# Macaron block: TensorE's implied waits left out of attention, and one quarter copy of v moved from ScalarE to VectorE

## The reference

```
qkv = x @ Wqkv.T + bqkv                       # x after a layer norm; 16 heads of 16
q = (elu(q) + 1 + 1e-4) / 4
k = elu(k) + 1 + 1e-4
num = q . cumsum(k v^T);  den = q . cumsum(k) + 1e-4
out = (num / den) @ Wout.T + bout             # then layer norm, gamma, beta
x = x + out
```

## Time and profile before

| | |
|---|---|
| time, median of 3 runs | 2193.14 us (2190.23 to 2194.28) |
| time of the profiled execution | 2192.45 us |
| its span, first to last instruction | 2190.7 us |
| granted TensorE clock, mean share of full speed | 0.994 |
| steps of attention read, 830 to 1394 us | 103 of 128 |

### The profile page before, as it was taken

One profiled execution on the slowest core, in us unless ns is written; L12 is line 12 of the kernel. 1 busy time (PEld: TensorE's weight loads), 2 busy tenths in 40 slices (PEclk: granted clock), 3 DMA queues, 4 the chain that ended last, 5 costly groups with the idle time before them and its releaser, 6 DMA issues.

```text
span 2190.7 us, 91337 instructions
## 1 busy us (share of the span) xinstructions
PE 2101.8 (96%) x30384; PEld 1506.7 (69%) x30384; DVE 2044.7 (93%) x5231; ACT 1930.6 (88%) x4136; POOL 1905.6 (87%) x3002
## 2 busy tenths in 40 slices
PE   3899999999999999999999999979999999999998
PEld 1566666666666688888888888864666666666665
DVE  7999999999999788999999999978999999999997
ACT  7888888888888789999999999978888888888885
POOL 5899999999999778888888888878999999999996
PEclk9999999999999999999999999999999999999999
DMA  4765555555555432222222222223555555555555
GB/s 103 130 121 117 116 115 116 115 115 114 114 114 110 85 57 59 61 61 61 61 61 61 61 61 61 61 45 72 121 115 116 116 114 114 114 114 116 115 119 116
DMA packets 719856, 208.74 MB, mean 95 GB/s; under 512 B 666400, under 2 KB 719520, under 8 KB 719776
## 3 DMA queue, kind: packets, MB, share of 16 engines
q1 hardware_dynamic: 719776, 207.76, 46.8%
HBM read 20.38 MB, written 16.78 MB: 17 GB/s over the span
## 4 chain that ended last, share of the span: by engine, by line
PE 88%; DVE 4%; issue 3%; ACT 2%; DMA 2%; POOL 1%; SPq 0%; POOLq 0%; ACTq 0%; DVEq 0%
PE ffn_ps_gu L861 39%; PE ffn_ps_down L873 21%; PE attn_ps_qk L1265 7%; PE attn_ps_sc L1318 5%; PE attn_ps_num L1305 4%; PE attn_ps_v_second L1281 3%; PE attn_ps_z L1345 3%; PE attn_ps_num L1310 2%; PE attn_ps_kT_first L1272 1%; PE attn_ps_z L1342 1%; PE attn_ps_kT_first L1333 1%; DMA attn_xT<-attn_x_hl 1%; DVE ffn_y L759 1%; DVE ffn_per_block L721 0%; PE attn_ps_v_second L1333 0%
## 5 line engine op out<-in xcount | busy, mean ns | idle before, releaser
L861 PE MATMUL ffn_ps_gu<-wgu_hi,ffn_xT 128*128 128x512 f16 (+1 forms) x3072 | 740.6, 364 | 14.5 <-DVE ffn_hx L710 6.2
L861 PEld LDWEIGHTS ffn_ps_gu<-wgu_hi,ffn_xT 128*128 128x128 f16 x3072 | 301.6, 98 | 302.4 <-issue 22.4
L861 PE MATMUL ffn_ps_gu<-wgu_lo,ffn_xT 128*128 128x512 f16 (+1 forms) x1536 | 432.9, 364 | 0.0
L791 POOL TENSOR_TENSOR ffn_h_hl<-ffn_q,ffn_h_scale_hi 128x704 f16<-128x704 f16 x256 | 352.5, 1377 | 28.2 <-DVE ffn_q L751 8.9
L807 ACT ACTIVATE ffn_quarter<-ffn_y,offsets 128x960 int16<-128x960 f32 (+2 forms) x264 | 282.5, 1070 | 99.2 <-DVE ffn_y L759 97.0
L873 PE MATMUL ffn_ps_down<-wd_hi,ffn_hT 128*128 128x256 f16 x2816 | 349.3, 273 | 10.0 <-DVE x_sb L735 6.0
L792 POOL TENSOR_TENSOR ffn_h_hl<-ffn_q,ffn_h_scale_lo 128x704 f16<-128x704 f16 x256 | 355.3, 1388 | 0.0
L873 PEld LDWEIGHTS ffn_ps_down<-wd_hi,ffn_hT 128*128 128x128 f16 x2816 | 274.5, 98 | 71.1 <-issue 9.4
L721 DVE TENSOR_REDUCE ffn_per_block<-ffn_hx 128x60 f32<-128x960 f32 (+2 forms) x264 | 298.0, 1129 | 5.4
L759 DVE TENSOR_TENSOR ffn_y<-ffn_hx,ffn_per_block 128x960 f32<-128x960 f32 (+2 forms) x264 | 292.4, 1108 | 0.0
L843 ACT ACTIVATE ffn_odd<-ffn_quarter,offsets 128x960 f16<-128x960 int16 (+2 forms) x264 | 278.7, 1056 | 10.8 <-POOL ffn_shift L786 10.8
(11 more groups left out here) (184 smaller groups left out, 5236.5 us busy)
## 6 DMA issues: line engine op xcount, KB each, us to landing
x_sb<-in_L_attn_x SPq DMA_DIRECT2D x128, 128.0 KB, 2.5
out<-x_sb SPq DMA_DIRECT2D x128, 128.0 KB, 2.1
attn_v_eo<-attn_v_nat SPq DMA_DIRECT2D x256, 34.0 KB, 1.8
ffn_xT<-ffn_x_hl SPq DMA_TRANSPOSE x256, 2.5
ffn_hT<-ffn_h_hl SPq DMA_TRANSPOSE x256, 3.5
attn_xT<-attn_x_hl SPq DMA_TRANSPOSE x128, 2.4
attn_oT<-attn_o_hl SPq DMA_TRANSPOSE x128, 2.5
x_sb<-in_L_ffn_w_gate SPq DMA_DIRECT2D x2, 352.0 KB, 5.0
```

The lines of the kernel that those rows point to most:

```text
L791: nc.gpsimd.tensor_tensor(blocks(h_hl[par][:, 0:INNER]), blocks(q[par][:, 0:INNER]), over_block(h_scale_hi[par][:], HB), ALU.mult)
L861: last = nc.tensor.matmul(ps_gu[par][:, a:b], xT[par][:, c, :], w[:, k, a:b], start=(n == 0), stop=(n == len(terms) - 1))
```

## The change

In TensorE's step most waits are left out where another wait of the same step implies them. Before `kT` the wait for `feat` stays only where no tile i + 1 exists. Before v the waits for `v_nat` and `kv_second` go. Before `num` ten waits (`mid`, `before`, `q_feat`, `placed`, `v_own`, `masked`, `o_ready`, `k_odd`, `q_rows`, `masked` of the tile before) become four, in the order `placed`, `mid`, `q_rows`, `masked`. Before `kv` the wait for `v_nat` and one increment of `turn` go. On ScalarE the quarter of the lower rows is copied no more, only that of the upper rows. VectorE makes the other copy, in front of `den`, and waits for `v_nat` of tile i + 1 and for `num_done` of the tile that used the buffer last.

```diff
@@ vector_step
                 nc.vector.scalar_tensor_tensor(zg[:], ps_z[:, 0:D], mv[oth][:, 2:3], rows[:, 1, :], ALU.subtract, ALU.mult).then_inc(S["z_gamma"], 1)
+            if valid(tf, N):
+
+                ready(dve, "v_nat", tf)
+                freed(dve, "num_done", tf, 2)
+                nc.vector.tensor_copy(v_eo[oth][half(0), 0, 0], v_nat[oth][half(0), 0]).then_inc(S["v_low"], 1)
             if valid(tm, N):
 
                 ready(dve, "num_done", tm)
@@ scalar_step
                 ready(act, "v_nat", tf)
                 freed(act, "num_done", tf, 2)
-                for a in range(2):
-                    last = nc.scalar.activation(v_eo[oth][half(a), a, a], v_nat[oth][half(a), a], ACT.Copy)
-                last.then_inc(S["v_own"], 1)
+                nc.scalar.activation(v_eo[oth][half(1), 1, 1], v_nat[oth][half(1), 1], ACT.Copy).then_inc(S["v_own"], 1)
@@ tensor_step
             if valid(i, N):
 
-                ready(pe, "feat", i)
+                if not valid(tf, N):
+                    ready(pe, "feat", i)
                 freed(pe, "kv_first", i, 1)
...
             if valid(tf, N):
 
-                if valid(i, N):
-                    ready(pe, "v_nat", i)
-                    if not (isinstance(i, int) and i == 0):
-                        pe.wait_ge(S["kv_second"], i)
                 for n, (aT, w, k) in enumerate(terms):
...
+                placed(pe, tn, oth)
                 ready(pe, "mid", tn)
-                if not (isinstance(tn, int) and tn == 0):
-                    pe.wait_ge(S["before"], tn)
-                ready(pe, "q_feat", tn)
-                placed(pe, tn, oth)
-                ready(pe, "v_own", tn)
+            if valid(i, N):
+                if not valid(tn, N):
+                    ready(pe, "k_odd", i)
+                ready(pe, "q_rows", i)
+            if valid(tn, N):
                 ready(pe, "masked", tn)
-                freed(pe, "o_ready", tn, 1)
-            if valid(i, N):
-                ready(pe, "k_odd", i)
-                ready(pe, "q_rows", i)
-                freed(pe, "masked", i, 1)
...
                 ready(pe, "k_nat", i)
                 pe.sem_inc(S["turn"], 1)
-                ready(pe, "v_nat", i + 1 if valid(tf, N) else i)
-                if not valid(tf, N):
-                    pe.wait_ge(S["kv_second"], N - 1)
-                pe.sem_inc(S["turn"], 1)
```

More of the change, by code:

```diff
@@ L879 @@
 ATTN_SEMS = ("sums", "stats", "var", "rstd", "shift", "xn", "x_hi", "x_split", "turn", "xT_even", "xT_odd", "qk_done", "relu", "exp", "feat", "k_even", "k_odd",
-             "q_feat", "q_rows", "v_done", "v_nat", "v_own", "v_eo_even", "v_eo_odd", "kT_done", "k_nat", "scores_done", "masked", "kv_done", "kv_first", "kv_second",
+             "q_feat", "q_rows", "v_done", "v_nat", "v_own", "v_low", "v_eo_even", "v_eo_odd", "kT_done", "k_nat", "scores_done", "masked", "kv_done", "kv_first", "kv_second",
              "mid", "before", "num_done", "den", "rden", "o_ready", "o_hi", "o_split", "oT_even", "oT_odd", "proj_done",
@@ L1286, in tensor_step @@
                     pe.wait_ge(F["y"], N + X_AHEAD)
+                placed(pe, tn, oth)
                 ready(pe, "mid", tn)
-                if not (isinstance(tn, int) and tn == 0):
-                    pe.wait_ge(S["before"], tn)
-                ready(pe, "q_feat", tn)
-                placed(pe, tn, oth)
-                ready(pe, "v_own", tn)
-                ready(pe, "masked", tn)
-                freed(pe, "o_ready", tn, 1)
-            if valid(i, N):
-                ready(pe, "k_odd", i)
-                ready(pe, "q_rows", i)
-                freed(pe, "masked", i, 1)
-            if valid(tn, N):
+            if valid(i, N):
[3 more added lines that the diff above has]
+            if valid(tn, N):
+                ready(pe, "masked", tn)
                 for c in range(DC):
```

## The result

The changed kernel takes 2199.79 us, median of 8 runs (2192.35 to 2204.41), against 2193.22 us for the kernel before, also 8 runs (2188.13 to 2194.79). The ratio is 1.0032, 95% interval 1.0021 to 1.0043: slower by 0.3%, where 2182 us was forecast. The profiled execution took 2199.45 us (span 2196.8).

A forecast was written before the change was run, and what follows sets the result against it. A dependence round through VectorE and the gap before `num` was the bound. Its new sum, 0.12 + 1.22 + 0.05 + 0.15 + 0.02 + 3.77 + 0.05 = 5.38, saves 10.4 us: 2192.45 to 2182, range 2170 to 2197.

The forecast's parts named there:

- The round of 5.47 us: Attention step before the change: gap after `masked` 0.43, `num` to `den` 1.22, `den` to `masked` 3.77, loop branch 0.05.
- Waits before `num`: TensorE ahead of `num`: gap after `masked` falls from 0.43 to 0.12 us, a gain of 0.31 a step.
- The copy's price: VectorE's copy ahead of `den`: 0.20 us a step, 0.05 for its wait and 0.15 start to start.
- The sum of 5.38: Attention step after the change, by the same round: 5.38 us, 0.09 less than before.
- The loop's term: VectorE's loop branch, ahead of `bn_stats`: 0.05 us a step.
- TensorE's 5.29 and ScalarE's 4.97: Attention step: TensorE's own floor, and ScalarE's busy time with one copy less, in us; both below the new step.
- the case that the rivals left at 0.05: A new stall, from the `oT` transposes or GpSimd's own round, on either side of the forecast; chance 0.05.
- the 115 steps: Steps counted as gaining 0.09 us each: the 103 read plus half of the other 25, 10.4 us in all.
- Rival C: GpSimd holds VectorE's copy by 0.22 us or all of `x_beta`: step 5.58, 13 us slower, 2205 us; chance 0.13.
- the 0.02 in the sum: Allowance in us a step for GpSimd holding up VectorE's copy ahead of `den`.
- "Hidden" waits: TensorE's waits left out before `kT`, v and `kv`, and one `turn` increment: worth zero, as matmuls still run meanwhile.
- ScalarE's relief: ScalarE loses one of two copies, 0.32 us a step: zero by itself, but removes what would have been the next bound.

The follow-up runs named there:

- before_oT_plain: The kernel before the change, with the DMA transpose of o replaced by a plain copy of the same tile: 2190.01 us, ratio 0.9988.
- waits_only: The changed kernel with ScalarE making both copies again, so only TensorE's waits are left out: 2182.92 us, ratio 0.9954.
- oT_plain: The changed kernel with the DMA transpose of o replaced by a plain copy of the same tile: 2182.20 us, ratio 0.9952.
- copy_only: The kernel before the change with one copy made by VectorE ahead of `den`, all of TensorE's waits kept: 2242.07 us, ratio 1.0219.
- no_low_copy: The changed kernel without VectorE's copy, so nobody copies that quarter of v and ScalarE makes one copy: 2185.75 us, ratio 0.9961.

## Why the prediction was wrong

**What bounds the kernel now: right.** The round of 5.47 us through VectorE and the gap ahead of `num` set the step before the change. before_oT_plain leaves the step at 5.48, so the other round was not in the way then.

**Waits before `num`: right.** The gap went from 0.43 to 0.14 or 0.15 (forecast 0.12) wherever `num` waits for `masked`. waits_only shows what this is worth, 10.5 us, together with the other waits left out.

**The copy's price: right in size.** The copy lasts 0.22 us, as the 225 ns of the prediction's working, and `den` starts 0.15 after the copy, as forecast; the estimate of 131 ns, which the prediction weighed against that 0.15, was 0.02 short. With the copy's wait, `num` to `den` grew from 1.22 (1101.75 to 1102.97) to 1.46 and 1.44 (1099.53 to 1100.99, 1104.89 to 1106.33), so by 0.22 to 0.24 where 0.20 was forecast.

**The sum of 5.38: right for the round it adds up.** oT_plain shows the changed kernel with the other round out of its way: 21.62 in four steps, 5.40 a step. That its time of 2182.20 us meets the forecast of 2182 as well is in part luck, since the same edit took 4 us from the kernel before without touching the step. The loop's term was a little small: `den` to the end of `masked` takes 4.03 in one step of four and 3.76 in the others, 0.07 a step for 0.05.

**The step that failed** is the sentence that followed: "It is still above TensorE's 5.29 and ScalarE's 4.97." The new round was held against the busy time of engines and not against other rounds of dependence. There was one, over four steps, through SyncE's queue and GpSimd. With waits and copy as changed it is 22.00 us long, 5.50 a step. In kind it is the case that the rivals left at 0.05 ("a new stall (the oT transposes, GpSimd's own round)") without a price. (22.00 - 21.62) / 4 = 0.095, and by the 115 steps that the prediction counts (its own estimate) this is 11 us of the 17.8 between forecast and result.

**Rival C came in part.** `x_beta` holds the copy, mostly by 0.6 us, in 7 of 128 steps, 3.9 us; this is 0.03 a step over all steps, near the 0.02 in the sum by luck, for nearly all other copies last 0.22. The prediction put the copy ahead of `shift`, and so of `x_beta`, which is true in three steps of four (1100.84 and 1101.16). In the fourth v is late, `num` is late with it, and the copy meets `x_beta` within 0.06 us. The number of held copies differs between the two profiled executions with the same steps otherwise (7 at 2199.45 us, 20 at 2207.71), so it can be a part of the spread of these kernels, 2192 to 2204 and 2192 to 2210 us. It isn't shown to be all: the kernel before, without this copy, spreads from 2188 to 2198 in 29 runs. The Trainium skill, "SBUF — State Buffer", section "Who interferes with whom", says that the order of issue decides which of the two is blocked; two pairs of rows agree: at 1155.86 the copy is first and `x_beta` takes 0.80 for 0.73, in copy_only `x_beta` is first by 0.08 (1065.71) and the copy takes 0.74 for 0.22. At 1265.84 the records begin 0.01 us apart, which is too close to tell from them which was issued first.

**What is left over.** Holds and the longer round make 15 of the 17.8 us; the rest was not taken apart. Between before and after as a whole, the steps from the 13th to the 121st `num` take 3.7 us more (834.35 to 1430.45 against 832.90 to 1425.33), the 12 steps ahead of them 1.2 and the 7 behind them 1.3.

**"Hidden" waits: right for this kernel, by luck.** They cost nothing in the changed kernel (22.01 against 22.00) and 0.16 in four steps without the copy. Why the longer kernel hides them and the shorter doesn't was not settled; they lie between qk and `num`, so they are a part of the round over four steps.

**ScalarE's relief: zero, as forecast,** but the remark that it "takes away what would have been the next bound" is wrong. no_low_copy has ScalarE at one copy and VectorE at none, and is no faster than waits_only.

## What to carry to other kernels

When a change shortens the round that sets the step, don't hold the new sum against busy times alone: start at the DMA issues and follow each loaded tile to its use and back to the issue, over as many steps as the loop unrolls, since here the waits of qk showed the round of four steps only once it had become the longest (one wait before the change, 51 after). Work moved onto an engine that stands in both rounds is paid in both; here the copy cost 17 us and the waits alone, at 2183 us, are the better kernel. And a fixed pattern of steps can put two operations that hold each other up at the same instant, so look at their distance in each step of the loop's body and not in one step or on average.

## What the runs showed of the hardware

- VectorE's copy of 64x136 f32 (0.22 us) and GpSimd's addition of 128x256 f32 (0.73 us) held each other up when they started together. With the addition first by 0.07 to 0.08 us (copy_only) the copy took 0.74; with the copy first by 0.02 to 0.03 the addition took 0.78 to 0.80. Within 0.01 us it went either way, with copies of up to 0.82.
- SyncE is busy 1.20 us for a transposing DMA of this tile and 0.48 us for a plain one; xT has landed 2.44 us after its issue starts (1083.60 in the changed kernel).
- A TensorE that the profile shows busy 563.76 of 564.00 us still had 0.07 us a step to give (5.40 to 5.33), once a transpose came earlier. Matmul ends are modelled in these records; the 45 waits of qk's weight loads for xT, 9.6 us, were the sign.
